# Graph attention on one Trainium2 core: the destination logits of an edge tile summed inside TensorE's accumulator

## The chip, the cores and the metric

The kernel runs on one core of a Trainium2 chip. The metric is the device time of one execution in microseconds (us), and less is better. Three runs of the kernel before gave 8301.24, 8236.3 and 8281.1 us, so the median is 8281.1 us. One further execution was taken with the hardware profiler. Its span, from the first to the last instruction, is 7531.3 us, and every row below is from it.

## The reference, cut to what matters

Two graph layers run over the same 12,500 nodes and 200,000 edges, which are sorted by destination. Only the first one, an attention layer with H = 4 heads, is touched:

```python
h = (x @ W).reshape(N, H, C)
a_src = jnp.einsum('nhc,hc->nh', h, att_src)
a_dst = jnp.einsum('nhc,hc->nh', h, att_dst)
e = a_src[src] + a_dst[dst]
e = jnp.where(e > 0, e, NEG_SLOPE * e)
e_max = jax.ops.segment_max(e, dst, num_segments=N)
alpha = jnp.exp(e - e_max[dst])
denom = jax.ops.segment_sum(alpha, dst, num_segments=N)
alpha = alpha / (denom[dst] + EPS)
msg = h[src] * alpha[:, :, None]
agg = jax.ops.segment_sum(msg, dst, num_segments=N)
```

`a_dst[dst]` and `e_max[dst]` are the eight numbers per edge that this case is about. The second layer turns an edge's attributes into radial weights by a small network of three layers, and sums weighted messages at the source nodes.

## The kernel before, in words

**Stages.** The program runs a preparation, then four stages, each written for all five engines as one software pipeline. Stage A, the attention stage, goes over the edges. Stage B is the node update, stage C the edges of the second layer, stage D the last node update. The change lies in stage A.

**Tiles of stage A.** The sorted edges are cut into T = 1664 tiles of 128 edges, each of which belongs to one block of 128 destination nodes. A step handles a group of GROUP = 4 tiles, so there are 416 steps. The function `steps` writes out the first and the last few steps, and runs the others in a loop whose body holds four steps, so that buffer slots are constants while tile numbers and wait values are held in registers. A tile's block number `b[k]` is a register too, so an operand such as `ac3[:, ds(b[k], 1), ...]` has an address that the engine's sequencer works out at run time.

**What a step does.** Step g works on several groups at once.
- POOL (L522) gathers the rows of h for four tiles, with the source logits behind them, into `hg`.
- DVE (L1204) makes the one-hot matrices `oh` (edge by node). TensorE transposes them in bf16 (L878, one for each tile), and ACT (L676) copies the transposes to `ots`.
- TensorE picks the destination's eight numbers for each edge: the transposed one-hot matrix is multiplied with the block's table `ac3`, which holds the fp32 values as three bf16 parts that add up to them. L871 multiplies all three parts at once: 24 columns for each tile, four instructions in a step, into PSUM bank 1.
- DVE adds the three parts (L1168, one reduction over 96 numbers per partition to 32, into the SBUF tile `ad`), then adds the source logits (L1178), makes the leaky maximum (L1078), subtracts the maximum (L1188) and clips (L1199). ACT takes the exponential (L658).
- DVE multiplies the rows with it (L1149, `message`, four in a step). TensorE sums the rows by node (L845, `sums`, four in a step), and DVE adds that to the block's accumulator in `big` (L1157, `add_up`, four in a step).
- TensorE also runs the small network for the second layer: L866 (first layer), L862 (second), L837 (third, two calls in a step), all in fp32. DVE finishes their activations (L1145) and ACT scales the result (L646, L648).

**Order.** It is written out by hand on each engine, and every hand-over is a semaphore. On TensorE a step is: third_layer(0), sums 0 and 1, third_layer(1), the load of the block numbers, sums 2 and 3, L862, L866, L871, L878. On DVE it is: messages 0 to 2, the reduction L1168, an activation, L1178, add_up 0, L1078, message 3, L1188, add_up 1, an activation, add_up 2, L1199, add_up 3, L1204. L871 waits for `s_z`, by which DVE says that bank 1 has been read; DVE's first reader waits for `s_ad`, which the last L871 of a group sets. A wait on TensorE may stand on the sequencer (its own instruction, L60), or be carried by a matrix instruction.

## Time and profile before

| what | value |
|---|---|
| median of three runs (lowest, highest) | 8281.1 us (8236.3, 8301.24) |
| span of the profiled execution | 7531.3 us |
| stage A in it, first to last L871 | 173.3 to 2582.3 us, 416 steps |
| busy share of the span: PE, DVE, ACT, POOL | 87%, 72%, 53%, 76% |

The time of a run is longer than the span, since it holds what lies before the first and behind the last instruction. PE is TensorE's matrix work, PEld its weight loads, PEldq what its sequencer does ahead of a weight load. The end of a matrix instruction in the profile is modelled and overlaps the next one's start, so the distance of two starts says more than a duration. A row of the timeline merges instructions of one line that follow each other; "x4" is their number.

### The profile page before, as it was taken

The numbers are of one execution on the slowest core, as the hardware profiler recorded it, in microseconds if no ns is written. First come the engines' busy times: TensorE is split into PE (matmuls) and PEld (weight loads), VectorE is DVE, ScalarE is ACT, GpSimd is POOL, SyncE is SP. The second block draws the span as 40 slices with busy tenths as digits, with TensorE's granted clock in tenths as the row PEclk, the third lists the DMA queues.
The fourth block names the chain that finished last, engine by engine and source line by source line (L and its number), as shares of the span: only waits on it lengthen the run. The fifth ranks groups of instructions, "written<-read, shape, count | busy, mean of one in ns | idle before, by whom it ended". The sixth has DMA issues, their size and how long they took to land.

```text
span 7531.3 us, 218435 instructions
## 1 busy us (share of the span) xinstructions
PE 6552.1 (87%) x36547; PEld 4301.1 (57%) x36548; DVE 5437.6 (72%) x20339; ACT 4022.4 (53%) x12733; POOL 5759.5 (76%) x4888
## 2 busy tenths in 40 slices
PE   6999999999999988888888888888888888888876
PEld 5666666666666555555555555555555555555544
DVE  3788888888888798666666666666666666666668
ACT  2455555555555455555555555555555555555532
POOL 3677777777777655888888888888888888888878
PEclk8899999999999999999999999999999999999999
DMA  5788888888888766777777777777777777777789
GB/s 178 200 224 223 224 225 224 222 224 226 224 223 223 207 221 192 136 136 135 136 135 135 136 136 136 136 135 136 135 135 137 136 136 135 136 136 135 136 227 299
DMA packets 1268411, 1312.20 MB, mean 174 GB/s; under 512 B 232303, under 2 KB 1153040, under 8 KB 1268272
## 3 DMA queue, kind: packets, MB, share of 16 engines
q0 software_dynamic: 368112, 577.39, 45.5%
q1 hardware_dynamic: 900258, 734.36, 33.8%
q8 instruction: 13, 0.21, 0.0%
q14 instruction: 28, 0.23, 0.0%
HBM read 723.28 MB, written 587.78 MB: 174 GB/s over the span
## 4 chain that ended last, share of the span: by engine, by line
PE 38%; issue 23%; POOL 19%; DMA 8%; DVE 7%; POOLq 2%; ACT 2%; DVEq 1%; ACTq 0%; SPq 0%
POOL part L571 13%; PE PS L845 12%; PE PS L837 12%; DMA part<-arena,c_idx 8%; POOL d_out L562 5%; PE PS L866 3%; PE PS L862 2%; PE PS L959 2%; PE PS L952 1%; PE PS L878 1%; ACT arena L724 1%; DVE arena L1310 1%; PE PS L871 1%; PE PS L789 1%; DVE arena L1298 1%
## 5 line engine op out<-in xcount | busy, mean ns | idle before, releaser
L571 POOL DMA_INDIRECT part<-arena,c_idx x1664 | 2671.4, 1605 | 515.8 <-issue 457.7
L522 POOL DMA_INDIRECT arena<-h_tab,sidx x1664 | 1773.8, 1066 | 634.9 <-issue 385.7
L1279 DVE SCALAR_TENSOR_TENSOR arena<-PS,c_src,lower_eq 128x128 f32<-128x128 f32 x1664 | 517.6, 348 | 1385.1 <-PE PS L964 1385.1
L717 ACT COPY arena<-PS 128x514 f32<-128x514 f32 x832 | 489.7, 589 | 1823.5 <-DMA part<-arena,c_idx 1823.3
L952 PE MATMUL PS<-ident,arena 128*128 128x128 f32 x3328 | 545.1, 286 | 679.7 <-ACT arena L724 666.5
L921 PEld LDWEIGHTS PS<-ident,arena 128*128 128x128 f32 x6656 | 739.8, 141 | 626.9 <-issue 582.7
L562 POOL DMA_INDIRECT d_out<-y_tab,c_row x832 | 829.2, 997 | 266.6 <-issue 252.6
L921 PE MATMUL PS<-ident,arena 128*128 128x128 f32 x6656 | 977.0, 280 | 61.5 <-issue 43.0
L710 ACT COPY arena<-PS 128x512 f32<-128x512 f32 x1664 | 991.7, 603 | 6.8 <-PE PS L921 6.7
L1157 DVE TENSOR_TENSOR big<-big,PS 128x260 f32 x1664 | 703.9, 423 | 396.2 <-PE PS L845 336.1
L845 PE MATMUL PS<-arena 128*128 128x260 f32 x3328 | 961.4, 412 | 3.5 <-DVE big L1157 2.2
L837 PE MATMUL PS<-fc,arena 64*128 64x256 f32 x3328 | 944.7, 405 | 0.0
L931 PE MATMUL PS<-arena,w2m 128*64 128x128 f32 (+1 forms) x6656 | 903.1, 392 | 0.4 <-ACT arena L710 0.4
L959 PE MATMUL PS<-arena 128*128 128x257 f32 x3328 | 860.6, 381 | 2.0 <-ACT arena L717 2.0
L952 PEld LDWEIGHTS PS<-ident,arena 128*128 128x128 f32 x3328 | 349.2, 140 | 867.2 <-ACT arena L724 863.9
L845 PEld LDWEIGHTS PS<-arena 128*128 128x128 f32 x3328 | 568.3, 190 | 332.3 <-issue 245.1
L837 PEld LDWEIGHTS PS<-fc,arena 64*128 64x128 f32 x3328 | 559.5, 187 | 234.7 <-ACT arena L648 116.0
L658 ACT ACTIVATE arena<-za 128x16 f32<-128x16 f32 x416 | 89.6, 215 | 1046.4 <-DVE za L1199 1046.4
L1149 DVE TENSOR_TENSOR arena<-arena 128x256 f32<-128x256 f32 x1664 | 625.9, 417 | 0.0
L959 PEld LDWEIGHTS PS<-arena 128*128 128x128 f32 x3328 | 569.2, 191 | 46.5 <-issue 2.4
L646 ACT ACTIVATE arena<-PS,sh 128x128 f32<-128x128 f32 x1664 | 513.3, 359 | 34.0 <-PE PS L837 8.0
L740 ACT COPY arena<-PS 128x512 f32<-128x512 f32 x832 | 513.0, 617 | 0.7 <-PE PS L952 0.7
(192 smaller groups left out, 11545.7 us busy)
## 6 DMA issues: line engine op xcount, KB each, us to landing
w_tab<-arena SPq DMA_DIRECT2D x416, 520.0 KB
arena<-w_tab SPq DMA_DIRECT2D x1664, 130.0 KB
part<-zeros SPq DMA_DIRECT2D x1664, 32.1 KB
arena<-part SPq DMA_DIRECT2D x392, 128.5 KB, 3.4
arena<-h_tab,sidx POOLq DMA_INDIRECT x1664
ot_tab<-arena SPq DMA_DIRECT2D x416, 64.0 KB
arena<-ot_tab SPq DMA_DIRECT2D x416, 64.0 KB
part<-arena,c_idx POOLq DMA_INDIRECT x1664
```

The source lines that it names most:

```text
L522: pool.indirect_dma_start(hg[:, s, k, :], None, h_tab, bass.IndirectOffsetOnAxis(ap=sidx[:, s, k:k + 1], axis=0)).then_inc(s_hg[s], 16)
L562: pool.indirect_dma_start(c_y[:, n // 2, k, :], None, y_tab, bass.IndirectOffsetOnAxis(ap=c_row[:, n // 2, k:k + 1], axis=0)).then_inc(s_c ...
L571: pool.indirect_dma_start(part[q], bass.IndirectOffsetOnAxis(ap=c_idx[:, s, k:k + 1], axis=0), o_cmb[:, q, :], None, compute_op=ALU.add).t ...
L710: a.copy(midT[:, m % 2, k, :, :], PS[:, T_BANK[k], :].rearrange("p (c e) -> p c e", c=4)).then_inc(s_cmT, 1)
L837: last = mm(PS[:, 4 + i, k * D:(k + 1) * D], h2[i * MUL:(i + 1) * MUL, o % 2, k * P:(k + 1) * P], fc3[i * MUL:(i + 1) * MUL, :], start=Tru ...
L845: mm(PS[:, 2 + k % 2, 0:HW], oh[:, p, k, :], hg[:, p, k, :], start=True, stop=True).then_inc(s_agg, 1)
L921: last = nc.tensor.transpose(PS[:, T_BANK[k], j * P:(j + 1) * P], mid[:, m % 2, k, 2 * j:2 * j + 2, :].rearrange("p c u -> p (c u)"), iden ...
L931: last = mm(PS[k * MUL:(k + 1) * MUL, 4, first * P:(first + n_comps) * P], w2m[:, min(first, 1), :], midT[:, s % 2, k, first:first + n_com ...
L952: last = nc.tensor.transpose(PS[:, 5, j * P:(j + 1) * P], oT_sb[:, j, :], ident[:, :])
L959: last = mm(PS[:, 6 + k, 0:OR], same[:, o, k, :], o_sb[:, o % 2, k, :], start=True, stop=True)
L1149: v.tensor_tensor(x, x, hg[:, o, k, D:HW].rearrange("p (h o) -> p h o", o=1).to_broadcast([P, H, C]), ALU.mult).then_inc(s_msg, 1)
L1157: v.tensor_tensor(x, x, PS[:, 2 + k % 2, 0:HW], ALU.add).then_inc(s_acc, 1)
```

## The change

The three parts are no longer laid side by side in PSUM. For each tile, three matrix products of 8 columns each, one for each bf16 part, go one after the other into the same eight numbers: the first (part 2) overwrites, the others (part 1, part 0) add. The reduction and its SBUF tile go away. DVE's addition and its subtraction read the eight numbers from PSUM bank 1. So `s_z` counts four steps and not five, DVE's wait for `s_ad` moves from the reduction to the addition, and TensorE's wait for bank 1 is for the subtraction of the group before, where it was for its reduction.

```diff
+        a_dst = PS[:, 1, 0:GROUP * 2 * H].rearrange("p (k j) -> p k j", k=GROUP)
-        ad = sb("ad", [P, 2, GROUP, 2 * H])
...
-                    wait(act, s_z, 5 * g)
+                    wait(act, s_z, 4 * g)
...
                 if there(g):
                     wait(pe, s_ots, g + 1)
-                    wait(pe, s_z, 5 * (g - 1) + 1)
+                    wait(pe, s_z, 4 * (g - 1) + 3)
                     for k in range(GROUP):
-                        last = mm(PS[:, 1, k * 6 * H:(k + 1) * 6 * H], ots[:, s % 2, k, :],
-                                  ac3[:, ds(b[k], 1), :, :].rearrange("p o i j -> p (o i j)"), start=True, stop=True)
+                        for i in (2, 1, 0):
+                            last = mm(a_dst[:, k, :], ots[:, s % 2, k, :],
+                                      ac3[:, ds(b[k], 1), i, :].rearrange("p o j -> p (o j)"), start=(i == 2),
+                                      stop=(i == 0))
                     last.then_inc(s_ad, 1)
...
-                if there(g - 1):
-                    wait(dve, s_ad, g)
-                    v.tensor_reduce(ad[:, m % 2, :, :],
-                                    PS[:, 1, 0:GROUP * 6 * H].rearrange("p (k i j) -> p k j i", k=GROUP, i=3),
-                                    AX.X, ALU.add).then_inc(s_z, 1)
...
                     wait(dve, s_hg[m], landed(g - 1, m, GROUP))
-                    wait(dve, s_z, 5 * g - 4)
-                    v.tensor_tensor(za[:, m % 2, :, :], hg[:, m, :, D:HW], ad[:, m % 2, :, 0:H], ALU.add).then_inc(s_z, 1)
+                    wait(dve, s_ad, g)
+                    v.tensor_tensor(za[:, m % 2, :, :], hg[:, m, :, D:HW], a_dst[:, :, 0:H], ALU.add).then_inc(s_z, 1)
...
-                    wait(dve, s_z, 5 * g - 2)
-                    v.tensor_tensor(za[:, m % 2, :, :], zb[:, m % 2, :, :], ad[:, m % 2, :, H:], ALU.subtract
+                    wait(dve, s_z, 4 * g - 2)
+                    v.tensor_tensor(za[:, m % 2, :, :], zb[:, m % 2, :, :], a_dst[:, :, H:], ALU.subtract
                                     ).then_inc(s_z, 1)
```

## Rows read from the trace of the kernel before

**Rows 1.** The page: span, and busy time of each engine, its share, instructions.
```profile
span 7531.3 us, 218435 instructions
PE 6552.1 (87%) x36547; PEld 4301.1 (57%) x36548; DVE 5437.6 (72%) x20339; ACT 4022.4 (53%) x12733; POOL 5759.5 (76%) x4888
```
**Rows 2.** Busy time by stage: preparation, A, B, C, D; the columns are the first line's.
```profile
core 0: us, PE busy (x) PEld busy (x) DVE busy (x) ACT busy (x) POOL busy (x), PEclk, DMA share, GB/s
0.00:171.00 171.00, 114.33 (x477) 93.16 (x478) 59.00 (x74) 45.81 (x207) 51.66 (x43) 0.89 0.56 182
171.00:2583.00 2412.00, 2406.15 (x11607) 1541.31 (x11608) 1974.57 (x6635) 1295.11 (x4964) 1772.71 (x1664) 0.99 0.85 221
2583.00:2860.00 277.00, 231.70 (x900) 147.92 (x899) 242.01 (x669) 133.45 (x379) 149.58 (x219) 0.96 0.67 212
2860.00:7200.00 4340.00, 3581.74 (x22655) 2363.04 (x22654) 2892.78 (x11838) 2464.88 (x6757) 3522.04 (x2553) 1.00 0.77 137
7200.00:7531.00 331.00, 218.16 (x915) 155.63 (x913) 269.22 (x1128) 83.17 (x429) 263.46 (x411) 0.94 0.90 281
```
**Rows 3.** The chain that ended last, 1000 to 1600 us, by line, and some pieces.
```profile
by line: PE PS L845 37.4%; PE PS L837 36.7%; PE PS L866 10.9%; PE PS L862 7.6%; PE PS L878 4.1%; PE PS L871 3.4%
...
1005.34 1.07 PE PS L845 x4
...
1597.59 1.07 PE PS L845 x4
```
**Rows 4.** Timeline of PE over one step: start us, us, engine, line, operation, count.
```profile
1005.27 1.15 PE L845 MATMUL PS<-arena 128*128 128x260 f32 x4
1006.25 0.59 PE L862 MATMUL PS<-arena,fc 128*128 128x256 f32 x2
1006.78 0.69 PE L866 MATMUL PS<-arena,fc 16*128 16x256 f32 x2
1007.40 0.26 PE L871 MATMUL PS<-ac,arena 128*128 x4
1007.52 0.38 PE L878 MATMUL PS<-ident_b,arena 128*128 128x128 bf16 x4
1007.83 1.13 PE L837 MATMUL PS<-fc,arena 64*128 64x256 f32 x4
1008.89 1.15 PE L845 MATMUL PS<-arena 128*128 128x260 f32 x4
1009.97 1.13 PE L837 MATMUL PS<-fc,arena 64*128 64x256 f32 x4
1011.02 0.49 PE L845 MATMUL PS<-arena 128*128 128x260 f32 x1
```
**Rows 5.** Timeline of DVE over the same step (the bracket: idle before, and releaser).
```profile
1007.71 1.09 DVE L1149 TENSOR_TENSOR arena<-arena 128x256 f32<-128x256 f32 x3
1008.72 0.26 DVE L1168 TENSOR_REDUCE ad<-PS 128x32 f32<-128x96 f32 x1
1008.89 0.41 DVE L1145 SCALAR_TENSOR_TENSOR arena<-arena,PS 128x256 f32<-128x256 f32 x1
1009.22 0.17 DVE L1178 TENSOR_TENSOR za<-arena,ad 128x16 f32<-128x16 f32 x1
1009.74 0.42 DVE L1157 TENSOR_TENSOR big<-big,PS 128x260 f32 x1 [0.36 <-PE PS L845]
...
1010.51 0.17 DVE L1188 TENSOR_TENSOR za<-zb,ad 128x16 f32<-128x16 f32 x1
1010.59 0.42 DVE L1157 TENSOR_TENSOR big<-big,PS 128x260 f32 x1
1010.93 0.41 DVE L1145 SCALAR_TENSOR_TENSOR arena<-arena,PS 128x256 f32<-128x256 f32 x1
```
**Rows 6.** DVE by line and shape, 1000 to 1600 us: busy us, mean ns | idle before.
```profile
L1157 DVE TENSOR_TENSOR big<-big,PS 128x260 f32 x418 | 176.8, 423 | 94.6 <-PE PS L845 79.2 <-issue 1.4
L1149 DVE TENSOR_TENSOR arena<-arena 128x256 f32<-128x256 f32 x417 | 156.9, 417 | 0.0
L1168 DVE TENSOR_REDUCE ad<-PS 128x32 f32<-128x96 f32 x104 | 26.3, 253 | 9.1 <-issue 9.0
```
**Rows 7.** L871 in one step; PEldq is sequencer work. Duration ns, first and last start.
```profile
L871 PEldq FUSED_REGOPS  x4: 46/48/51, 1006.1 to 1006.5; - x4
L871 PE MATMUL PS<-ac,arena x4: 173/173/187, 1007.4 to 1007.5; 128*128 x4
```
**Rows 8.** Two lines with run-time addresses: DMA L383 (1000 to 1600 us), copy L609.
```profile
L383 SPq DMA_DIRECT2D part<-zeros x420: 327/373/991, 999.6 to 1599.2; - x140
...
L383 SPq FUSED_REGOPS  x104: 46/46/46, 1004.8 to 1597.5; - x104
...
L609 ACT COPY logits<-PS x98: 171/171/296, 37.6 to 147.0; 128x8 f32 x84, 128x8 f32<-128x8 f32 x14
L609 ACTq FUSED_REGOPS  x84: 46/46/52, 74.2 to 146.7; - x84
```
**Rows 9.** Clock from 152 to 230 us, and the timeline of PE inside that stretch.
```profile
152.00:230.00 78.00, 57.78 (x165) 34.37 (x165) 41.16 (x114) 18.52 (x65) 40.24 (x38) 0.50 0.40 100
...
174.37 0.28 PE L871 MATMUL PS<-ac,arena 128*128 x4
174.50 0.59 PE L878 MATMUL PS<-ident_b,arena 128*128 128x128 bf16 x4
```
**Rows 10.** L778, eight-column fp32 products that add up in PSUM, in the preparation.
```profile
L778 PEld LDWEIGHTS PS<-att,WTs x8: 289/333/337, 29.4 to 30.8; 128*128 128x128 f32 x8
L778 PE MATMUL PS<-att,WTs x8: 361/361/383, 29.4 to 30.9; 128*128 128x8 f32 x8
```

More of the change, by code:

```diff
@@ L1181, in step_a @@
                 if there(g - 1):
-                    wait(dve, s_z, 5 * g - 3)
+                    wait(dve, s_z, 4 * g - 3)
                     leaky(zb[:, m % 2, :, :], za[:, m % 2, :, :]).then_inc(s_z, 1)
@@ L1196, in step_a @@
                 if there(g - 1):
[L1198 removed]
+                    wait(dve, s_z, 4 * g - 1)
                     v.tensor_scalar(za[:, m % 2, :, :], za[:, m % 2, :, :], 0.0, None, ALU.min).then_inc(s_z, 1)
```

1 line of the change is left out of this document (removed).

## The prediction

> **What bounds the kernel now.** I read the page first. PE is busy for 87% of the span, the highest share, but the stages differ [rows 1]. The busy time by stage shows that in stage A PE is busy 2406 of 2412 us, at the full clock but for the start (mean 0.99), while DVE has 1975 and POOL 1773 [rows 2]. Stages B, C and D do not run the changed lines, so their 4948 us stay as they are.
>
> In the middle of stage A the chain that ended last consists of PE alone. Its pieces repeat: from 1005.34 to 1597.59 us lie 592.25 us, which is 103 times 5.75 us [rows 3]. The timeline of PE shows the period once, 1005.27 to 1011.02, with each line beginning as the one before ends [rows 4]. 416 steps of 5.75 us are 2392 us, nearly the whole stage. So a step costs what PE puts into it. DVE waits 94.6 us in 600 ahead of L1157, mostly for PE's L845, and never makes PE wait [rows 6]. Whatever DVE saves becomes a longer wait there.
>
> **What the change removes.** L1168 is 253 ns on DVE [rows 6], from its start to the next one's 0.17 us [rows 5]. It stands between message 2 and the activation of the first layer. Behind these comes the wait of 0.36 us for L845 ahead of add_up 0 [rows 5]. The 0.17 us fall into that wait. Value on the path: 0. If that cover were missing, the gain would be 416 x 0.17 = 71 us.
>
> **What it moves.** TensorE's wait for bank 1 is now for L1188. On DVE that is ahead of add_up 1 (1010.51 against 1010.59), and TensorE's sums(3), which stands ahead of L871 in its queue, waits for add_up 1 already. So the new wait is always met when it is reached: 0. Without that order L871 would be held, and L878 and third_layer behind it. DVE's wait for `s_ad` is for a group that PE finished in the step before (1007.5, needed at 1009.2): 0. The two DVE operations now read PSUM. 256 numbers from SBUF (L1149) take 417 ns and 260 with a PSUM operand (L1157) take 423 [rows 6], which is the same per number, so I add 0. A supplement of 60 ns on L1188 would delay add_up 1 and, by the argument on the sequencer below, count for at most that, 25 us in all; none is the lower end, since a gain from PSUM has no row.
>
> **What it adds on the array.** Twelve instructions of 8 columns replace four of 24, that is eight more in a step. Four of 24 columns take 0.12 us from the start of L871 to that of L878, 30 ns each; four of 128 take 0.31, 78 ns, with a change of array shape behind them [rows 4]. Is the 30 ns set by columns or by something fixed? In the stretch at clock 0.50 (1.2 GHz) the four still take 0.13 us [rows 9]. Had columns or weights set it, the time would have doubled. So it is fixed, and 8 columns cost as much as 24. The upper bound is 30 ns for each of the eight: 240 ns, 100 us. The lower bound lets columns count fully. 104 columns fewer save 78 - 30 = 48 ns, so 16 fewer save 7 ns, and each costs 23: 12 x 23 - 4 x 30 = 156 ns; with a steeper slope, all of the 78 ns put down to the 128 columns, 16 save 10 ns, and it is 120 ns, 50 us. I take 25 ns for each of the eight, nearer to the fixed end but below 30, since the first of the four in the row follows a change of the array's shape (16 rows to 128) and may bear some of the 0.12 us for itself. Added: 8 x 25 = 200 ns a step, 416 x 0.2 = 83 us.
>
> The Trainium skill has a rule against the change here ("TensorE: Matmul & The Clock Gate", section "Wait — 56ns, not 53.3ns?"): however few columns a matmul has, starts lie at least about 25 ns apart. By it the array's part, an estimate, is 8 x 25 = 200 ns a step. The trace's 0.12 us for four at the full clock and 0.13 at half agree; what 8 columns do no row shows.
>
> Adding into PSUM could cost more than overwriting, if an instruction had to see the sum of the one before it. L778 adds 8-column products. Its eight lie 1.5 us / 7 = 0.21 us apart, with a duration of 361 ns each [rows 10]. So an adding product starts before the one before it has ended, and I take 0. Whether that holds at 25 ns, no row shows; a full wait of 173 ns [rows 7] for each of eight would be the far end, 416 x 8 x 0.148 = 492 us.
>
> **What it adds on the sequencer.** Each L871 has a register operation for its address, four in a step, 1006.1 to 1006.5, so 0.13 us apart, with the weight load and the product in between [rows 7]. Will there be twelve? L383 issues four DMAs with one offset into four tensors and has one register operation for them (104 for 420), but L609, whose run-time index has a different constant each time, has 84 for its 84 looped copies [rows 8]. The three parts of `ac3` share the block number and differ by a constant, like L609. I take twelve.
>
> The array reaches L871 at 1007.40, 1.3 us after the first register operation: the sequencer is ahead. Twelve operations end at 1006.1 + 11 x 0.13 = 1007.5, and the array, at 25 ns each, takes its last at 1007.40 + 0.28 = 1007.7. So L871 itself is still fed in time. Behind it the sequencer has the waits for `s_ots` and `s_oh` ahead of L878: two operations more. At 0.13 each L878 can begin at about 1007.8, while the array would be free at 1007.72. Then come two more for third_layer(0), met at about 1008.1 on both sides. So the array stands still for about 0.09 us in a step. It is not made good elsewhere. L862 waits for DVE's L1145 behind add_up 1, which in this step ended at 1011.34 - 5.75 = 1005.59 [rows 5], and the first register operation comes 0.5 us later, three waits on. That L1145 follows PE's own sums, so the sequencer's lead is set anew in each step and does not grow. Bounds: 0 with four register operations; 0.2 us with slots of 0.14 and an additional one.
>
> **Sum.** 0.20 + 0.09 = 0.29 us a step. 416 x 0.29 = 121 us. On the profiled span that is 7531 + 121 = 7652 us. The median of the runs is 750 us above the span, time outside of it that the change leaves alone: 8281 + 121 = 8402, rounded 8400 us, 1.4% slower. DMA (share 0.85) and POOL only get more time for each step.
>
> **The rivals.**
> - *The sequencer stays ahead*: four register operations, or more lead than I read. Only the array's 0.20 us remain, 8281 + 83 = 8364 us, 1.0% slower. For it: the lead of 1.3 us, and L383. Against it: L609.
> - *Columns count after all*: 120 ns, 8331 us. Against it: the half-clock rows.
> - *The sequencer is the bound of the block, or sums wait*: twelve slots of 0.13 us replace 0.12 us of array time. If most of the eight additional ones, 1.04 us, come to light, say 0.6 us, the time is 8281 + 250 = 8530 us. For it: register operations cost five times the array's spacing. Against it: the lead. The same page and section of the Trainium skill say that with hardware decoding off a matmul takes the sequencer about 62 ns. By that rule, an estimate, eight more would take it 0.5 us a step, 206 us where nothing hides them; the trace's slots of 0.13 us, each with a product in it, leave it open.
> - *The other side: PE's additional work is hidden and DVE's relief counts.* PE may have holes: L866's two products hold it for 0.62 us, L862's two of the same 256 columns for 0.53 [rows 4]. If small products could fill such holes, and DVE's 0.17 us would come out: 8281 - 71 = 8210 us. It decides if the period is set by DVE. Against it: 5.75 us to the digit for 103 periods, and DVE's waits for L845.
> - *No difference*: the holes are filled, and nothing is gained: 8281 us.
>
> **How the numbers follow.** About 1% is what a measurement of this kernel can tell from no change. Chances: my case 0.45 (with its own range 8370 to 8440), sequencer ahead 0.25, columns count 0.08, sequencer or sums as the bound 0.10, hidden and no difference 0.08, faster 0.04. The range goes from 8325, so that "columns count" is in, to 8460, nearly my case's upper bounds together (0.24 + 0.2 us a step, 8464); left out are the two hidden cases and the larger part of the slow one. Slower by over 1% (8364 and up): 0.45 + 0.10 + half of 0.25, about 0.68. Faster by over 1%: 0.03. Within: 0.29.
>
> **What would show it.** L871 x12 in a step, its first start to that of L878 0.32 us or more; twelve register operations 0.13 us apart; a hole ahead of L878; a period of 6.04 us (5.95 by the first rival, 6.35 by the third, 5.75 or less by the last two); DVE's wait ahead of add_up 0 up from 0.36 to about 0.5 us; L1178 and L1188 still near 168 ns; PE's other lines spaced as before. I am wrong if the period stays at 5.75, or if a place other than L871 and L878 grows.

## The result, and the profile after

The kernel after takes 8287.66 us (median of 17 runs, 8268.15 to 8306.78), the kernel before, run beside it, 8250.18 us (17 runs, 8178.85 to 8301.24). The ratio is 1.0043, with an interval from 1.0023 to 1.0063: 0.4% slower. The prediction, 8400 us with a range from 8325 to 8460, is too high. The direction is right, and the loss is a third of the 121 us that were forecast.

The page and the stages of the profiled execution of after (columns of the windows as in [rows 2]; the middle row is stage A, the last one 600 us out of it):

```profile
span 8271.6 us, 227599 instructions
PE 6986.4 (84%) x39875; PEld 4530.2 (55%) x39876; DVE 5419.1 (66%) x19923; ACT 4099.1 (50%) x12733; POOL 5840.6 (71%) x4888
...
0.00:171.00 171.00, 113.34 (x477) 91.67 (x478) 60.93 (x73) 45.86 (x207) 51.40 (x43) 0.87 0.56 182
171.00:3218.00 3047.00, 2824.87 (x14972) 1770.19 (x14974) 1962.60 (x6241) 1319.48 (x4982) 1738.00 (x1664) 0.92 0.65 175
1000.00:1600.00 600.00, 556.51 (x2998) 349.62 (x2997) 393.02 (x1253) 264.66 (x1001) 349.78 (x333) 0.94 0.66 178
```

This execution took 8273.99 us, so time and span differ by 2 us. Its span is 740 us longer than that of [rows 1], which a change of some 40 us can't explain. The cause is in the comparison, not in the change: stage A takes 3047 us against 2412 in [rows 2], and PE, which was busy nearly all of it (2406 of 2412 us), is busy 93%. The first experiment profiled the kernel before once more, on another chip, and got this (the same three views; here the windows are stage A and the same 600 us):

```profile
span 8292.9 us, 218435 instructions
PE 6971.3 (84%) x36547; PEld 4445.6 (54%) x36548; DVE 5439.4 (66%) x20339; ACT 4110.9 (50%) x12733; POOL 5814.1 (70%) x4888
...
171.00:3233.00 3062.00, 2812.59 (x11646) 1688.88 (x11646) 1986.88 (x6657) 1330.39 (x4988) 1706.36 (x1664) 0.88 0.65 175
1000.00:1600.00 600.00, 552.17 (x2335) 331.11 (x2333) 396.45 (x1332) 265.06 (x999) 341.63 (x334) 0.90 0.66 177
```

So the same program has two sets of times, and which one it shows goes with the chip. On two chips (11 and 8) the kernel before took 7528.6 and 7527.9 us; I call them **quick**. The profile ahead of the prediction, 7531.3 us, shows what they show. On three (14, 3 and 9) it took 8244.6, 8258.9 and 8215.3 us; I call them **stretched**, and the runs with the median of 8281.1 us, and the 17 above, lie there. The sessions came in the order 14, 11, 3, 8, 9, so the two kinds took turns; but no chip was used in two sessions, and whether a chip stays of its kind is not shown. In the sum, a step from a quick chip was added to a median from stretched ones.

What differs is seen in L60 and L317, the sequencer's own instructions (waits, register operations, loads of block numbers). Columns: duration in ns, least, median and longest; first and last start. First the kernel before on the quick chip, then on the stretched one, 1000 to 1600 us:

```profile
L60 DVEq ALU_OP  x808: 40/40/45, 1000.4 to 1598.5; - x162
L317 PEldq SEQ_ASSERT  x416: 18/18/18, 1003.6 to 1596.7; - x139
```
```profile
L60 DVEq ALU_OP  x645: 4/40/721, 1002.7 to 1599.1; - x162
L317 PEldq SEQ_ASSERT  x332: 3/18/697, 1006.1 to 1597.2; - x166
```

The medians are the same; on the stretched chip some of these operations last up to 0.72 us. It happens on PE, DVE and SP; ACT's waits of L60 last 17 ns without exception on both. In the count of such **long operations** I leave out the loads of block numbers (TENSOR_LOAD, over 300 ns on either chip) and what SP does for its DMA issues (DMA_DIRECT2D, MOVE). Between 300 and 2500 us 163 operations of PE, 175 of DVE and 313 of SP then last over 250 ns on the stretched chip, and none does on the quick one. On the quick chip a step of before is 5.75 us. On the stretched one it is 6.66 us where the clock is full, for PE waits ahead of sums 2 and once more between sums 2 and 3 (timeline of PE, two periods of one step; the bracket is idle time and its releaser):

```profile
1031.07 1.13 PE L837 MATMUL PS<-fc,arena 64*128 64x256 f32 x4
1032.12 1.14 PE L845 MATMUL PS<-arena 128*128 128x260 f32 x4
1033.20 1.13 PE L837 MATMUL PS<-fc,arena 64*128 64x256 f32 x4
1034.78 0.68 PE L845 MATMUL PS<-arena 128*128 128x260 f32 x2 [0.45 <-DVE big L1157]
1035.62 0.68 PE L845 MATMUL PS<-arena 128*128 128x260 f32 x2 [0.17 <-issue]
1036.13 0.59 PE L862 MATMUL PS<-arena,fc 128*128 128x256 f32 x2
```

The add_up that it waits for begins late on DVE, and behind that wait stands a long sequencer operation of DVE itself (timeline of DVE, then L60 and L1157 in 1032.2 to 1034.4 us):

```profile
1034.21 0.42 DVE L1157 TENSOR_TENSOR big<-big,PS 128x260 f32 x1 [1.80 <-PE PS L845]
```
```profile
L60 DVEq ALU_OP  x2: 40/368/695, 1032.4 to 1034.2; - x2
L60 DVEq EVENT_SEMAPHORE  x1: 14/14/14, 1033.1 to 1033.1; - x1
```
```profile
L1157 DVEq FUSED_REGOPS  x1: 57/57/57, 1034.1 to 1034.1; - x1
```

The name in the bracket is PE's L845, but PE had begun those sums at 1032.12 and the next line at 1033.20. One ALU_OP of 695 ns (40 otherwise) lies in the 1.80 us. Behind it and the short operation at 1033.1 comes nothing on DVE's sequencer until 1034.1: about 1 us in which the profile shows no operation at all. So the delay stands in the records partly as a long operation and partly as a gap.

After on a stretched chip, one step (the line numbers moved by one or two: L872 the small products, L880 the transposes, L1159 add_up, L1175 the addition, L1185 the subtraction):

```profile
1099.88 0.50 PE L872 MATMUL PS<-ac,arena 128*128 x12
1100.42 0.38 PE L880 MATMUL PS<-ident_b,arena 128*128 128x128 bf16 x4
1100.73 1.13 PE L837 MATMUL PS<-fc,arena 64*128 64x256 f32 x4
1101.79 1.14 PE L845 MATMUL PS<-arena 128*128 128x260 f32 x4
1102.87 1.13 PE L837 MATMUL PS<-fc,arena 64*128 64x256 f32 x4
1104.51 1.11 PE L845 MATMUL PS<-arena 128*128 128x260 f32 x4 [0.52 <-issue]
1105.46 0.59 PE L862 MATMUL PS<-arena,fc 128*128 128x256 f32 x2
```

L872 to L880 is 0.54 us, where L871 to L878 was 0.12 in [rows 4]. Of the two waits at the sums one is left. Over all steps outside stretches of low clock the step grows from 6.66 to 6.90 us. (All such means and medians here are worked out from the starts of PE's instructions in stage A, from one step ahead of the first L871 to the stage's end. A step is outside if no stretch at 1.2 GHz, a **fall** of the clock, touches it or ended less than 5 us before it.) The part from L872's start to third_layer(0) takes 0.60 us more, sums 0 and 1 take 0.07 more, and what lies between third_layer(1) and L866, with the waits at sums 2 and 3, takes 0.44 less.

### The profile page after: what moved, and what is told of

Same layout as the page of the kernel before. It is cut to its first block, busy times and chain, and to the rows that moved or that the text cites. A ratio compares the mean times of both kernels' runs of the same rounds, so it can differ in the third digit from the quotient of the medians.

```text
span 8271.6 us, 227599 instructions
## 1 busy us (share of the span) xinstructions
PE 6986.4 (84%) x39875; PEld 4530.2 (55%) x39876; DVE 5419.1 (66%) x19923; ACT 4099.1 (50%) x12733; POOL 5840.6 (71%) x4888
## 4 chain that ended last, share of the span: by engine, by line
PE 37%; issue 28%; POOL 17%; DVE 7%; DMA 4%; ACT 2%; another core or an unknown queue 1%; POOLq 1%; DVEq 1%; ACTq 0%; SPq 0%
POOL part L571 11%; PE PS L845 11%; PE PS L837 10%; POOL d_out L562 4%; DMA part<-arena,c_idx 4%; PE PS L866 3%; PE PS L862 2%; PE PS L872 2%; PE PS L961 2%; PE PS L880 2%; PE PS L954 1%; PE PS L923 1%; PE PS L933 1%; PE PS L789 1%
## 5 line engine op out<-in xcount | busy, mean ns | idle before, releaser
L571 POOL DMA_INDIRECT part<-arena,c_idx x1664 | 2787.1, 1675 | 514.6 <-issue 460.8
L522 POOL DMA_INDIRECT arena<-h_tab,sidx x1664 | 1738.9, 1045 | 1293.5 <-PE PS L845 910.2
L845 PE MATMUL PS<-arena 128*128 128x260 f32 x3328 | 1065.0, 441 | 143.4 <-issue 98.5
L710 ACT COPY arena<-PS 128x512 f32<-128x512 f32 x1664 | 979.1, 595 | 195.4 <-PE PS L923 165.1
L837 PE MATMUL PS<-fc,arena 64*128 64x256 f32 x3328 | 1009.0, 427 | 57.1 <-issue 56.6
L1159 DVE TENSOR_TENSOR big<-big,PS 128x260 f32 x1664 | 705.0, 424 | 533.0 <-PE PS L845 350.3
L845 PEld LDWEIGHTS PS<-arena 128*128 128x128 f32 x3328 | 590.2, 203 | 566.5 <-issue 495.9
L837 PEld LDWEIGHTS PS<-fc,arena 64*128 64x128 f32 x3328 | 594.4, 198 | 325.9 <-issue 224.7
L676 ACT COPY arena<-PS 128x512 bf16<-128x512 bf16 x416 | 243.5, 585 | 930.8 <-remote 872.3
L961 PEld LDWEIGHTS PS<-arena 128*128 128x128 f32 x3328 | 569.9, 191 | 45.4 <-issue 1.1
L724 ACT COPY arena<-PS 128x512 f32<-128x512 f32 x832 | 489.0, 588 | 96.1 <-remote 59.9
```

The lines of the kernel that those rows point to most:

```text
L522: pool.indirect_dma_start(hg[:, s, k, :], None, h_tab, bass.IndirectOffsetOnAxis(ap=sidx[:, s, k:k + 1], axis=0)).then_inc(s_hg[s], 16)
L571: pool.indirect_dma_start(part[q], bass.IndirectOffsetOnAxis(ap=c_idx[:, s, k:k + 1], axis=0), o_cmb[:, q, :], None, compute_op=ALU.add).t ...
L710: a.copy(midT[:, m % 2, k, :, :], PS[:, T_BANK[k], :].rearrange("p (c e) -> p c e", c=4)).then_inc(s_cmT, 1)
L837: last = mm(PS[:, 4 + i, k * D:(k + 1) * D], h2[i * MUL:(i + 1) * MUL, o % 2, k * P:(k + 1) * P], fc3[i * MUL:(i + 1) * MUL, :], start=Tru ...
L845: mm(PS[:, 2 + k % 2, 0:HW], oh[:, p, k, :], hg[:, p, k, :], start=True, stop=True).then_inc(s_agg, 1)
L961: last = mm(PS[:, 6 + k, 0:OR], same[:, o, k, :], o_sb[:, o % 2, k, :], start=True, stop=True)
```

## The experiments

Theories under test: **S**, that the two sets of times belong to two kinds of chips, and that nothing lies outside the span; **R**, that the cost of the change is the twelve register operations of L872 on PE's sequencer, with the array's 25 ns for each further product; **C**, that what PE does with its time alters the granted clock, so that a busier array gets part of its cost, or more, back. Each kernel was run beside the kernel before on the same chip. Ratios are to that, with 95% intervals. The texts of what was expected use letters of their own and say what each means. Those of e5, e6, e7 and e8 give times for a stretched chip, but all four ran first on a quick one, where 8206 or 8290 us can't come out; there only the ratio and the step are of use.

### Which chip: before again, after again

> The kernel before, unchanged. Its first profile had a span of 7531 us with a step of 5.75 us in stage A, while its timed runs have a median of 8250 us. Theory P (the 720 us lie outside the profiled span, as the prediction had it): the span is again near 7531 us, some 720 us below the time of the same execution. Theory S (the first profile caught a rare, faster course of stage A): span and time agree within 5 us, near 8250 us, and stage A takes about 3000 us, 7.2 us a step, with idle time on PE and stretches of the lower clock.

The kernel before, unchanged, on chip 14: 8294.61 us, span 8292.9 (rows above). Span and time agree within 2 us, so nothing of the 750 us lies outside the span. Stage A has 650 of the 762 us by which this span is longer than that of [rows 1] (3062 against 2412), stages C and D have the rest.

> The changed kernel again, beside the kernel before on the same chip. So far the kernel before took 8250 us on one chip, where register operations of the PE, DVE and SP sequencers last up to 0.72 us, and 7529 us on another, where none lasts over 0.21 us. Theory K (the prediction's sum holds where PE sets the step, and is covered where it does not): on a chip of the second kind the step goes from 5.75 to 6.10 us, of which 0.20 are the array, 0.09 a hole ahead of L880 and 0.07 the loop's end, and with some falls of the clock the kernel is 2.5 to 3.5% slower, 7715 to 7790 us; on one of the first kind 0.4% slower. Theory L (the change costs the same few tens of us everywhere): +0.4% on both.

After, unchanged, on chip 3: 8309.81 us against 8258.87, ratio 1.0064 [1.0036, 1.0093]. Step away from low clock 6.90 us, as in the first profile of after.

> The changed kernel beside the kernel before. Two kinds of chips have shown: on two of them the kernel before takes 8250 us and sequencer operations of PE, DVE and SP last up to 0.72 us; on a third it takes 7529 us and none does. On a chip of the second kind: 2.5 to 3.5% slower, 7715 to 7790 us, step 6.10 us between falls of the clock. On one of the first kind: +0.4 to +0.7%.

After, unchanged, on chip 8, a quick one: 7799.67 us against 7527.93, ratio **1.0361 [1.0344, 1.0378]**, 272 us slower. The text expected 7790 us at most for a quick chip, so this is a little more. The change costs 3.6% on one kind of chip and 0.4 to 0.6% on the other. Stage A and the 600 us of this run, and one step (both views as above):

```profile
171.00:2874.00 2703.00, 2674.71 (x14974) 1725.55 (x14974) 1912.47 (x6241) 1349.62 (x4984) 1779.12 (x1664) 0.94 0.76 198
1000.00:1600.00 600.00, 594.47 (x3345) 383.76 (x3346) 426.45 (x1393) 301.47 (x1115) 397.18 (x372) 0.95 0.76 199
```
```profile
1004.10 0.46 PE L872 MATMUL PS<-ac,arena 128*128 x12
1004.58 0.38 PE L880 MATMUL PS<-ident_b,arena 128*128 128x128 bf16 x4
1004.89 1.13 PE L837 MATMUL PS<-fc,arena 64*128 64x256 f32 x4
...
1010.22 0.46 PE L872 MATMUL PS<-ac,arena 128*128 x12
1010.68 0.39 PE L880 MATMUL PS<-ident_b,arena 128*128 128x128 bf16 x4
1011.29 1.12 PE L837 MATMUL PS<-fc,arena 64*128 64x256 f32 x4 [0.23 <-issue]
```

PE is busy 99% of the stage, so here it does set the step, as the prediction had it. The clock fell, though: 0.94 over the stage, where [rows 2] have 0.99.

### Products without their addresses: e3

```diff
-    ac3[:, ds(b[k], 1), i, :].rearrange("p o j -> p (o j)"), start=(i == 2),
+    ac3[:, k:k + 1, i, :].rearrange("p o j -> p (o j)"), start=(i == 2),
```

The change with a constant address, that is, without register operations (the block of the table is left out of the computation).

> The changed kernel with constant addresses in the twelve products, so that the sequencer has no register operations for them (each tile uses the table of one of the first four blocks and not of its own, so the logits are not those of its block). If the sequencer's twelve operations are what costs: faster than the changed kernel by at least the 0.4% that the change costs, and probably faster than the kernel before, 8180 to 8250 us. If the array's time of the eight products is: no difference to the changed kernel, 8290 us.

Chip 14: 8257.06 us, 1.003 [0.9994, 1.0066].

> The changed kernel with constant addresses in the twelve products (each tile uses the table of one of the first four blocks), as before. Where PE sets the step: theory K says that the hole and the loop's end go, the step is 5.95 us and the time 7529 + 83 = 7612 us, +1.1%, with no fall of the clock in the middle of stage A. If the hole has another cause than the register operations, the step stays at 6.10 us and the time near that of the changed kernel. On a chip of the first kind: +0.3%, as measured.

Chip 3: 8239.69 us, 0.9977 [0.9952, 1.0002]. No difference to before is shown. On this chip after took 8309.81 us, 1.0064 [1.0036, 1.0093]: without the run-time addresses the same twelve products take 70 us less, clear of noise. Of that, 0.11 us a step (6.78 and 6.79 us, 6.90 in after) are 46 us; the rest goes with a higher clock (median of the runs 0.964, after 0.957). On chip 14 the gain is not shown, since after was not run there. These are stretched chips, so this is what R costs where part of it is hidden; on a quick chip this version was not run.

### DVE's half alone: e2

```diff
-                        for i in (2, 1, 0):
-                            last = mm(a_dst[:, k, :], ots[:, s % 2, k, :],
-                                      ac3[:, ds(b[k], 1), i, :].rearrange("p o j -> p (o j)"), start=(i == 2),
-                                      stop=(i == 0))
+                        last = mm(PS[:, 1, k * 6 * H:(k + 1) * 6 * H], ots[:, s % 2, k, :],
+                                  ac3[:, ds(b[k], 1), :, :].rearrange("p o i j -> p (o i j)"), start=True, stop=True)
...
```

Four products of 24 columns as before; the reduction is gone, and DVE reads from PSUM. Parts 1 and 2 of the logits are left out of the computation.

> DVE's half of the change alone: four products of 24 columns a step as before, no reduction, and the two DVE operations read only the first of the three bf16 parts from PSUM (the other two parts are left out of the logits). Theory A: no difference to the kernel before, within 0.3%. Theory B: faster by 0.17 us in each of 416 steps, 71 us, -0.9%, about 8180 us.

Chip 14: 8205.78 us, 0.9942 [0.9913, 0.9971].

> DVE's half alone again: four products of 24 columns, no reduction, and DVE reads the first of the three bf16 parts from PSUM (the other two are left out). Where PE sets the step: 0.0%, 7529 us, step 5.75 us, since the reduction stood ahead of DVE's wait for PE. If DVE's relief counts there too: -0.5% or more, as on the first chip.

Chip 3: 8237.46 us, 0.9982 [0.9951, 1.0014]. The step is 6.67 and 6.68 us, that of before 6.66. By the two intervals DVE's relief is worth at most 0.9%, and by the second it may be nothing; the steps at full clock don't show it. With the clock of each run taken into account (the straight line in the sum for stretched chips below), both sets of runs lie where those of before do, at most 3 us from the line. So no gain but that of the clock is shown, and whether the clock was higher by chance stays open.

### TensorE's half alone: e1

```diff
+                        for i in (1, 0):
+                            last = mm(PS[:, 1, (12 + 2 * k + i) * 2 * H:(13 + 2 * k + i) * 2 * H], ots[:, s % 2, k, :],
+                                      ac3[:, ds(b[k], 1), i, :].rearrange("p o j -> p (o j)"), start=True, stop=True)
```

Before, with two more 8-column products for each tile into an unused part of the bank. They were meant to bring eight register operations. The trace shows four more: the product with i = 0 has the address of the one of 24 columns and shares its register.

> The kernel before with TensorE's half of the change alone: behind each tile's product of 24 columns come two more of 8 columns into unused columns of the same bank, and the reduction stays. Theory A (TensorE's extra work is what costs, DVE's relief gives nothing): the same as the changed kernel, +0.4%, about 8290 us. Theory B (two effects that nearly cancel): +1 to +1.5%, 8330 to 8370 us, more than the changed kernel.

Chip 14: 8206.17 us, 0.9951 [0.9927, 0.9976].

> The kernel before with two further products of 8 columns behind each one of 24, the reduction kept. One of the two shares the 24-column product's address, so there are eight register operations a step (four before, twelve in the changed kernel) for the same twelve products. Where PE sets the step, theory R: eight operations are done before the array needs them, so 5.95 us a step and 7528 + 83 to 110 us, 7611 to 7640 us, like the kernel with three tables and not like the changed kernel (7800 us). Theory A: near 7800 us, as the changed kernel. On a chip with stretched sequencer operations: 8206 us, -0.5%, as measured.

Chip 9: 8177.95 us, 0.9961 [0.9934, 0.9988]. The text expected it slower, by 0.4% or by 1 to 1.5%, and both theories missed: eight additional products in a step make the kernel *faster*, twice, on stretched chips. Outside low clock the step is longer (6.87 and 6.88 us against 6.66). The gain is in the clock: 241 and 262 us of stage A lie at the low level, against 754 in the profile of before (its span is 8292.9 us, more than most runs of before on that chip take). The timed runs say the same: 0.967 to 0.981 in them, 0.945 to 0.968 in those of before. That speaks for C.

### A busier array, nothing else: e8

```diff
+                        last = mm(PS[:, 1, 128:256], ots[:, s % 2, k, :], ident_b[:, :], start=True, stop=True)
```

Before, with one more product of 128 columns for each tile, at a constant address: no register operation, nothing for DVE.

> The kernel before with one product of 128 columns more for each tile, four in a step, into unused columns of the same bank; nobody reads them. By the spacing of L878 they hold the array for 4 x 55 = 220 ns a step, 91 us in all. Theory C: the clock rises well above 0.954, to 0.97 to 0.98, and the time falls by more than the 91 us would cost, to 8150 to 8210 us. Theory D: the clock stays at 0.954, and the time is 8250 to 8340 us.

Chip 11 (quick): 7619.81 us against 7528.63, 1.0122 [1.0105, 1.0139], +91.2 us.

> The kernel before with four products of 128 columns more a step, whose result nobody reads; no register operation more. On the chip where PE sets the step it cost 91 us, as the array's spacing says, with no fall of the clock in the middle of stage A. On a chip with stretched sequencer operations, theory C (a busier array keeps its clock): clock above 0.965 in place of 0.954, and 8150 to 8230 us, faster than the kernel before. If the clock is not what gives time back there: 8250 to 8340 us.

Chip 8 (quick): 7616.45 us, 1.0118 [1.0101, 1.0135]. Step 5.97 us, which is 5.75 + 0.22, and 416 x 0.22 = 92 us. Where PE sets the step, array time costs itself, no more and no less, and the clock is whole (here without those falls):

```profile
171.00:2678.00 2507.00, 2499.31 (x13310) 1635.69 (x13310) 1980.67 (x6658) 1341.25 (x4988) 1783.25 (x1664) 0.99 0.81 214
```

> The kernel before with four products of 128 columns more a step, no register operation more. Where PE sets the step: +1.2%, as measured twice. On a chip with stretched sequencer operations, theory C (a busier array keeps its clock there): clock above 0.965 in place of 0.954 and 8150 to 8230 us. If the clock gives nothing back: 8250 to 8340 us.

Chip 9 (stretched): 8129.24 us against 8215.31, **0.99 [0.9856, 0.9943]**. The very edit that costs 1.2% on a quick chip gains 1.0% here:

```profile
171.00:3078.00 2907.00, 2685.94 (x13310) 1646.65 (x13310) 1966.83 (x6658) 1312.59 (x4988) 1709.32 (x1664) 0.96 0.69 184
```

The stage's clock is 0.96 against 0.88 in the profile of before on a stretched chip (chip 14); on chip 9 itself, the whole execution has 0.978 to 0.982 in these four runs and 0.946 to 0.968 in the 19 of before. The step away from low clock costs 0.10 us more (6.77 against 6.66), and 227 us lie at the low level, against 754. C holds on stretched chips.

### What costs 272 us on a quick chip: e6, e5, e7, e10

```diff
+                if there(g - 1):
+                    v.tensor_reduce(ad[:, m % 2, :, :],
+                                    iota_n[:, 0:GROUP * 6 * H].rearrange("p (k i j) -> p k j i", k=GROUP, i=3),
+                                    AX.X, ALU.add)
```

e6 is after with a reduction of the old size back in DVE's order (over other data, its result unused).

> The changed kernel with a reduction of the same size put back at its old place on DVE; it reads a constant from SBUF, and nobody uses its result. Theory D: like the kernel with eight products added and the reduction kept, 8206 us and clock 0.973. Theory C: the reduction is hidden, 8290 us and clock 0.961, like the changed kernel.

Chip 11: 7798.54 us, 1.035 [1.0305, 1.0395]. After itself has 1.0361, so the reduction is worth nothing where PE sets the step.

```diff
-    ac3[:, ds(b[k], 1), i, :].rearrange("p o j -> p (o j)"), start=(i == 2),
+    ac3[:, ds(b[k], 1), i:i + 2, :].rearrange("p o i j -> p (o i j)"), start=(i == 2),
```

e5 is after with products of 16 columns (the table has a fourth part, a copy of part 0; the additional columns are computed and not read; the edits that make room for it are not shown).

> The changed kernel with each of the twelve products 16 columns wide and not 8: the table holds the parts as 0, 1, 2, 0, so that the three products still add all three parts into the first eight numbers; nothing is left out. A product's distance to the next stays 25 ns. Theory C (how much the array streams decides how often its clock falls, and so the time): the mean granted clock rises from 0.961 towards the 0.973 of the kernel with eight products added, and the time falls to 8200 to 8240 us. Theory D (the columns are idle matter; DVE's order or the waits made the difference of the two): clock 0.961 and 8290 us, like the changed kernel.

Chip 11: 7747.62 us, 1.0305 [1.0281, 1.0329]. Step 6.139 us, that of after is 6.141: twice the columns cost nothing. The gain to after, some 50 us (after ran on the other quick chip), is in the clock: 106 us low, against 327.

```diff
-                        last = mm(PS[:, 1, k * 6 * H:(k + 1) * 6 * H], ots[:, s % 2, k, :],
-                                  ac3[:, ds(b[k], 1), :, :].rearrange("p o i j -> p (o i j)"), start=True, stop=True)
+                        for i in range(3):
+                            last = mm(PS[:, 1, (3 * k + i) * 2 * H:(3 * k + i + 1) * 2 * H], ots[:, s % 2, k, :],
+                                      ac3[:, ds(b[k], 1), i, :].rearrange("p o j -> p (o j)"), start=True, stop=True)
```

e7 is before with its products split in three, side by side as they were: no adding in PSUM, DVE untouched.

> The kernel before with each product of 24 columns split into three of 8 that lie side by side in PSUM, as many columns as before, and the reduction kept: the change's number of products without its adding in PSUM, without its DVE half and with the old wait. Theory C: like the changed kernel, 8270 to 8300 us, clock 0.96. Theory D: like the kernel with eight products added, 8206 us, clock 0.973.

Chip 11: 7751.04 us, 1.0293 [1.0276, 1.031]. The split alone costs 222 us; after cost 272 on the other quick chip.

```diff
-        ac3 = sb("ac3", [P, NB, 3, 2 * H], BF16)
+        ac3 = [sb(f"ac3_{i}", [P, NB, 2 * H], BF16) for i in range(3)]
...
-                                      ac3[:, ds(b[k], 1), i, :].rearrange("p o j -> p (o j)"), start=(i == 2),
+                                      ac3[i][:, ds(b[k], 1), :].rearrange("p o j -> p (o j)"), start=(i == 2),
...
```

e10 is after with the three parts in three tables. It was meant to leave four register operations a step where after has twelve, since a tile's three addresses now have one run-time offset. The trace shows something else: four FUSED_REGOPS and eight ALU_OP, so still one operation for each product, but a shorter one (32 ns for 46) for two of three. First e10, then after, both on chip 8, 1000 to 1600 us:

```profile
L872 PE MATMUL PS<-ac,arena x1188: 165/167/181, 1005.4 to 1596.9; 128*128 x198
L872 PEldq ALU_OP  x792: 32/32/32, 1004.3 to 1596.6; - x198
L872 PEldq FUSED_REGOPS  x396: 46/46/56, 1004.1 to 1596.4; - x198
```
```profile
L872 PEldq FUSED_REGOPS  x1116: 42/46/70, 1002.8 to 1599.1; - x186
L872 PE MATMUL PS<-ac,arena x1116: 165/167/188, 1004.1 to 1599.2; 128*128 x186
```

> The changed kernel with the three bf16 parts in three tables of their own, so that the three products of a tile share one register operation: twelve products, four register operations a step as before, nothing left out. Theory R (the eight additional register operations are what costs beside the array's 0.2 us): on a chip where PE sets the step, 5.95 us a step and 7529 + 83 = 7612 us, +1.1%, with few falls of the clock; on one with stretched sequencer operations faster than the changed kernel by 0.5 to 1.5%, and no slower than the kernel before. Theory A (the array's products alone cost): like the changed kernel on either chip.

Chip 8: 7634.66 us, 1.0142 [1.0125, 1.0159], +107 us. The same twelve products adding in PSUM, with other addresses, cost 165 us less. That is not because operations are gone, but because they follow each other sooner. In the mean of the steps outside falls, the twelve lie 0.121 us apart in e10, 0.129 in e7 and 0.132 in after, so the last comes 11 x 0.011 = 0.12 us earlier in e10 than in after. From L872 to L880 (L879 in e7) it is 0.329, 0.408 and 0.444 us: 0.115 us less in e10 than in after, which is the same. So on quick chips the pace of the sequencer sets the hole, and R holds with its mechanism; that the array's part is there in all three kernels leaves it no rival for the hole. Of the 165 us, the step's 0.11 us are some 46; the rest goes with the falls of the clock, of which e10 has none in mid-stage. Why they come and go with the hole is not shown. One step of e10:

```profile
1005.42 0.46 PE L872 MATMUL PS<-ac,arena 128*128 x12
1005.77 0.38 PE L880 MATMUL PS<-ident_b,arena 128*128 128x128 bf16 x4
1006.08 1.13 PE L837 MATMUL PS<-fc,arena 64*128 64x256 f32 x4
```

> The changed kernel with three tables, four register operations a step, again. Where PE sets the step: 7635 us, +1.4%, as measured. On a chip with stretched sequencer operations, theory R: 0.5% or more below the changed kernel's +0.4 to +0.6%, so no slower than the kernel before (8250 us); the PE sequencer's long operations fall from 410 in stage A to the 160 of the kernel before. Otherwise: +0.4%.

Chip 9 (stretched): 8256.26 us, 1.0033 [1.0005, 1.0061]; after has 1.0043 and 1.0064. The intervals overlap, so no gain over after is shown, where 0.5% or more was expected. PE has 417 long operations here as in after, where 160 were expected. The step is 6.885 us, after's 6.89 and 6.90. This does not speak against R here: the trace has twelve operations of the sequencer in both, 0.125 us apart in e10 and 0.135 in after, and no version with four of them and twelve products was made.

### The sequencer's bound checks: e9

```diff
             return nc.values_load_multi_w_load_instructions(
-                row[:, ds(at, n)], engines=(eng.engine,), min_val=0, max_val=below - 1)[1]
+                row[:, ds(at, n)], engines=(eng.engine,), min_val=0, max_val=below - 1,
+                skip_runtime_bounds_check_because="the rows are counts, clamped from above where they are made")[1]
```

Before, without the run-time checks (SEQ_ASSERT) on the block numbers, one for each tile and engine.

> The kernel before without the sequencers' checks on loaded block and window numbers (the numbers are clamped where they are made; nothing of the result is left out), which takes four of some thirty sequencer operations from each step of PE and of DVE. Where PE's array sets the step: no difference, 7529 us. Where sequencer operations are stretched and PE waits for its sequencer ahead of L845: faster by 0.1 us a step or more, 8150 to 8210 us in place of 8250.

Chip 3: 8298.64 us, 1.003 [0.9997, 1.0062]. A gain was expected for a stretched chip, and none is shown; the step is 6.66 us, as before. The trace says more. Of L317 only this is left of the two engines, so eight operations a step are gone from each, four SEQ_ASSERT and four FUSED_REGOPS:

```profile
L317 DVEq FUSED_REGOPS  x78: 53/53/75, 1000.0 to 1590.0; - x78
L317 PEldq FUSED_REGOPS  x78: 42/42/46, 1001.6 to 1591.6; - x78
```

With them went nearly all long operations of these engines: none of PE and 7 of DVE last over 250 ns, where before had 163 and 175 (SP keeps 249 of 313). Yet PE waits at the sums just as long: 1.52 us from third_layer(1) to sums 2 and 1.34 from there to L862, 1.51 and 1.32 in before. So the long operations of PE and DVE are not by themselves what lengthens the step; what is left are loads of block numbers that last up to 1.2 us, SP's operations, and gaps between the records, like the one at 1033.1 us above. With the clock taken into account, these runs lie 28 us under the line of before (see the sum for stretched chips), but their mean clock is lower, 0.941 against 0.953 in those of before on this chip. So the removal may gain something that the clock takes away.

## Why the prediction was wrong, and where it was right

Two steps of the prediction failed. The one that put it out of its range is the last addition, by which the trace's 5.75 us a step and a cost of 0.29 us a step were carried over to runs on chips where PE does not set the step; there the change costs 37 to 51 us. The other is the sum itself, 121 us. It is a sum for a quick chip, and there the change costs 272 us: its array term and its zeros for DVE and PSUM held, the hole was too small, and two terms were missing, the loop's end and the clock. That the direction is right on stretched chips is in part luck, since most of what decides it there, the waits that shrink and the clock that rises, isn't in the prediction. Point by point:

- **"The median of the runs is 750 us above the span, time outside of it that the change leaves alone."** Wrong. The time is 2 us above the span. The difference is in the stages: in the profile of before on chip 14 it is 762 us, 650 of them in stage A (3062 against 2412). This step carried the forecast of a quick chip over to runs on stretched ones. The 7531.3 and 8281.1 us side by side should have been read as a warning that they do not belong together.
- **"A step costs what PE puts into it."** Right on quick chips (e8: 92 us by its array time, 91.2 measured). Wrong on the others: there PE stands still for 0.9 us a step (6.66 - 5.75), and these waits take up 0.44 of the 0.60 us that the change adds from L872 to third_layer(0).
- **"Whatever DVE saves": 0.** Right on quick chips (e6 against after: 1.035 and 1.0361). On stretched ones between 0 and 0.9% (e2), and nothing where runs at the same clock are compared.
- **PSUM operands and adding: 0.** Right in size. L1175 takes 171 ns in after, L1178 took 167 (medians). e7, without adding, is within 50 us of after. Outside falls its step is 6.10 us and that of after 6.14, some 18 us in all, which its shorter slots on the sequencer explain (0.129 and 0.132 us apart); the rest is in the falls of the clock, 205 us in e7. The medians of the step by loop position, 6.37, 6.00, 6.10 and 6.09 us for after, are 6.35, 5.95, 6.05 and 6.07 for e7.
- **25 ns on the array for each of eight more.** Right. e10, where the sequencer's twelve slots end in time, goes from 0.114 to 0.329 us for L872 to L880, +0.215. "Columns count" fell: the e5 step with twice the columns is the same. So the rule quoted from the Trainium skill ("TensorE: Matmul & The Clock Gate", section "Wait — 56ns, not 53.3ns?"), that starts lie at least about 25 ns apart however few the columns, agrees with the trace. Its 62 ns for the sequencer no run here shows by itself; a product with an address worked out at run time takes the sequencer 0.13 us, with its register operation and its weight load (in e7 twelve FUSED_REGOPS begin from 1001.893 to 1003.315 us, and 1.422 / 11 = 0.129).
- **Twelve register operations.** Right (1116 for 1116 products). But the rival's argument from L383, four DMAs on one register operation, was read off lines that leave one out: the same view has 419 MOVE for the 420 DMAs. In e10 the products that should have shared one have an ALU_OP each. **The hole of 0.09 us.** The mechanism is right and the size too small: L872 to L880 is 0.444 us on average against 0.114 in before, +0.33, which is 0.20 for the array and 0.13 for the hole.
- **The lead "is set anew in each step".** Not in every step: once in each turn of the loop, behind L880's waits, PE's sequencer has a branch (COMPARE_BRANCH, 208 ns, at 1010.82 us in the trace of a_third). In before its lead covers that, and the four positions of the loop all take 5.75 us. Now the lead is used up, third_layer(0) is late there (the 0.23 us in the rows of a_third), and that position takes 6.37 us where the others take 6.0 to 6.1. On average over the steps L880 to L837 grows from 0.314 to 0.379 us, +0.065. With the +0.33 that is the 0.39 us of the sum below.
- **The clock.** Put at nothing, without a reason. The profile of before on a quick chip had 64 us at 1.2 GHz in stage A, all at its start. After on a quick chip falls to it 22 times in mid-stage; with the start it is 327 us in all.

The sum for the quick chip: outside the falls the step goes from 5.75 to 6.14 us, 415 steps x 0.39 = 162 us, where 121 were predicted. The 63 steps in or just behind the falls take 8.39 us, 63 x (8.39 - 6.14) = 141 us, less 24 us that the start of before had of the same, +118. Together 280. From the first L871 to the last, before takes 2408 us and after 2688 from the first L872, which is 280 too, and the time grew by 272.

The sum for stretched chips: outside the falls 6.66 to 6.90 us, 416 x 0.24 = 100 us, nearly the forecast, though by other terms. The steps in or just behind falls were 107 in before, each 2.66 us too long (284 us), and are 87 or 104 in after, each 2.0 us too long (174 and 208 us). So 76 to 110 us come back, as C says. These are single profiles, and they don't add up to the 37 to 51 us measured, but to between -10 and 24 us; the profile of before is one of its slower runs (8294.61 us, where the median there is 8244.6).

The timed runs give a better sum, since the granted clock of each is on record. In 74 runs of before on chips 14, 3 and 9 the time lies on a straight line over the clock, 6.0 us less for each 0.001 more, with 7 us of scatter; in 27 runs of after it does so too, with the same slope. At a clock of 0.960 the lines stand at 8212 and 8293 us, so at the same clock the change costs 81 us. But the mean clock is 0.9598 in after and 0.9546 in before, and that gives 31 us back. What is left is 50 us, within what was measured. The line shows that time and clock go together, not which of them moves the other.

Of the rivals, "hidden" is what a stretched chip does with most of the cost, though by two mechanisms that it did not name; "the sequencer is the bound" is nearest to the quick chip's +272 us with its 250, but not for its reason: it had 0.6 us a step, and 0.39 were measured; the rest is the clock.

**Open.** What makes chips 14, 3 and 9 slow: nothing in these traces names it. Why PE has more than one long operation a step there with the change, on average (417 and 410 in 2200 us in after's two profiles and 417 in e10, 163 in before). The counts go with the number of sequencer operations that work out the small products' addresses in a step: 4 and 7 long ones with none (e3), 134 to 163 with four (before, e2, e8), 180 and 142 with eight (e1), 410 to 417 with twelve. But the three profiles with twelve also have DVE's new order, and e7, with twelve and the old one, ran only on a quick chip, so the two are not separated; and e9, with four, has none. Why the clock falls in mid-stage on a quick chip in after, e5, e6 and e7 and not in before, e8 and e10. No version was found that is faster than both kernels on both kinds of chip. e8 beats both on stretched ones and loses to before on quick ones.

## What to carry to other kernels

Check that the profile's span and the times that you must forecast belong together before you add one to the other; where they differ by a tenth, the first question is what the slower machine waits for. On instructions with a run-time address count the sequencer's time, not only the array's: here each took a slot of 0.12 to 0.13 us there and 0.025 on the array, and 0.01 us less for each slot made the array wait 0.12 us less in a step. Look at the operations in the trace too, since what is meant to share one may still have its own, as in e10. And measure on more than one chip an edit that loads or relieves TensorE: the same 91 us of array work cost 1.2% on one kind and gained 1.0% on the other.

## What the runs showed of the hardware that was not expected

- Chips of the same type run one program at 7528 and 8250 us. On the slower ones short sequencer operations of PE, DVE and SP last up to 0.72 us now and then (18 to 40 ns otherwise), those of ACT never over 0.07. But with these gone from PE and DVE (e9) the step is as long.
- Three products whose addresses have one run-time offset into three tables had one FUSED_REGOPS (46 ns) and two ALU_OP (32 ns) on PE's sequencer, 0.121 us apart; as slices of one table they had three FUSED_REGOPS, 0.132 us apart. Two products with the very same address had one operation (e1).
- The granted clock falls to 1.2 GHz and comes back within stage A although PE hardly rests: in after on a quick chip PE is 99% busy, and the clock falls 22 times. In e8 and e10 on such chips, whose PE is busy with hardly a hole ahead of the transposes, it doesn't fall in mid-stage at all. Page section 2 of the two, mean clock in slices of 1/40 of the span, after and then e10 on chip 8:

```profile
PEclk8899999999999989999999999999999999999999
```
```profile
PEclk8999999999999999999999999999999999999999
```

- On stretched chips more array work means a higher clock: 0.88 in stage A for before, 0.92 for after, 0.96 for e8, and the time follows it.
